# First two groups' maxima taken key part by key part; first keys and queries laid out ahead of the second keys

## What is computed

```python
q, k, v = (t.reshape(B, S, 16, 16) for t in (ln(x) @ Wq.T, ctx @ Wk.T, ctx @ Wv.T))   # 2048 queries, 1601 keys, 256 wide
scores = q k^T / 4, masked keys and future keys (key > query) at -inf
context = nan_to_num(softmax(scores)) @ v
x = x + (sigmoid(ln(x) @ Wg.T + bg) * context) @ Wo.T
x = x + sum over 8 experts of top-2 gated silu(xs @ w1) * (xs @ w3) @ w2,   xs = gate * ln(x)
```

## Time and profile before

| | |
|---|---|
| median of 3 runs | 688.75 us (688.59 to 693.32) |
| the profiled execution | 690.36 us, its span 688.6 us |
| mean granted PE clock of it | 0.963 |
| PE, DVE, ACT, POOL busy | 653.8, 469.9, 385.0, 242.9 us |

### The profile page before, as it was taken

The page is one execution under the profiler, slowest core; times in us unless marked ns, Lnnn a source line. Parts: engine busy times, 40 slices in busy tenths (PEclk is TensorE's granted clock), DMA queues, the critical chain, the costliest instruction groups (busy, mean ns, idle before and its releaser), DMA issues.

```text
span 688.6 us, 13557 instructions
## 1 busy us (share of the span) xinstructions
PE 653.8 (95%) x5320; PEld 377.0 (55%) x5320; DVE 469.9 (68%) x969; ACT 385.0 (56%) x778; POOL 242.9 (35%) x293
## 2 busy tenths in 40 slices
PE   7897999999989999999999999999999996899996
PEld 3354455455545445444554445545456675688884
DVE  5684778999866999989987975454423354645452
ACT  2212676766634777777566877677875640232331
POOL 5004123422140305020211614527164535566563
PEclk9898999999996999999999999999999998899997
DMA  6984766010700000000770101003010011012000
GB/s 169 242 118 84 130 129 79 2 21 33 114 11 1 3 3 2 2 33 32 96 181 1 35 1 31 2 3 108 2 44 21 16 33 62 31 62 90 34 31 30
DMA packets 29305, 36.58 MB, mean 53 GB/s; under 512 B 5833, under 2 KB 16457, under 8 KB 29242
## 3 DMA queue, kind: packets, MB, share of 16 engines
q1 hardware_dynamic: 26248, 34.53, 23.7%
q10 hardware_dynamic: 946, 0.92, 0.4%
q0 software_dynamic: 2048, 0.27, 0.3%
HBM read 25.58 MB, written 8.06 MB: 49 GB/s over the span
## 4 chain that ended last, share of the span: by engine, by line
PE 74%; POOL 9%; DVE 7%; issue 6%; ACT 4%; POOLq 0%; ACTq 0%; DVEq 0%
PE bank L1566 18%; PE bank L1544 14%; PE bank L1511 11%; PE bank L1395 11%; PE bank L1630 3%; POOL h_lo L1022 3%; POOL v_sb L1018 3%; PE bank L1632 2%; PE bank L1631 2%; DVE pmax L1284 2%; POOL xn_sb L994 2%; ACT probs L1150 2%; PE bank L1515 2%; DVE v_sb L1374 2%; PE bank L1470 2%
## 5 line engine op out<-in xcount | busy, mean ns | idle before, releaser
L1284 DVE TENSOR_REDUCE pmax<-bank 128x1 f32<-128x512 f32 (+6 forms) x640 | 327.5, 578 | 69.3 <-PE bank L1515 46.8
L1150 ACT ACTIVATE probs<-bank 128x512 f32<-128x512 f32 (+4 forms) x592 | 287.4, 545 | 138.0 <-PE bank L1544 86.8
L1566 PE MATMUL bank<-probs,vaug 128*32 128x256 f32 (+4 forms) x2048 | 156.1, 396 | 0.5 <-ACT probs L1150 0.5
L1544 PE MATMUL bank<-qaug,kaug 64*128 64x512 f32 (+4 forms) x592 | 149.0, 452 | 7.0 <-DVE pmax L1284 3.2
L1511 PE MATMUL bank<-kaug,qaug 62*128 62x512 f32 (+6 forms) x640 | 139.6, 414 | 3.1 <-DVE pmax L1284 1.6
L1544 PEld LDWEIGHTS bank<-qaug,kaug 64*128 64x128 f32 (+1 forms) x592 | 64.4, 185 | 82.3 <-ACT probs L1150 29.8
L1511 PEld LDWEIGHTS bank<-kaug,qaug 62*128 62x128 f32 x640 | 70.7, 189 | 56.5 <-DVE pmax L1284 21.3
L1032 POOL TENSOR_SCALAR nmax<-rmax 128x16 f32<-128x16 f32 x16 | 5.2, 323 | 235.3 <-DVE rmax L1292 235.3
L1566 PEld LDWEIGHTS bank<-probs,vaug 128*32 128x32 f32 (+1 forms) x2048 | 46.5, 109 | 52.1 <-issue 31.1
L1202 ACT ACTIVATE h_hi<-v_sb 128x512 fp32r<-128x512 f32 x32 | 20.2, 632 | 80.5 <-DVE v_sb L1374 79.4
L1022 POOL TENSOR_TENSOR h_lo<-v_sb,h_hi 128x512 fp32r<-128x512 f32 x32 | 41.2, 1288 | 61.3 <-ACT h_hi L1202 61.3
(11 more groups left out here) (137 smaller groups left out, 790.2 us busy)
## 6 DMA issues: line engine op xcount, KB each, us to landing
qaug<-s_dram SPq DMA_DIRECT2D x32, 256.0 KB, 3.3
qaug<-q_parts SPq DMA_DIRECT2D x18, 256.0 KB, 9.2
q_parts<-stage SPq DMA_DIRECT2D x7, 512.0 KB, 2.9
k_parts<-stage SPq DMA_DIRECT2D x4, 512.0 KB, 5.3
w_sb<-in_w SPq DMA_DIRECT2D x4, 512.0 KB, 11.0
out<-x_sb SPq DMA_DIRECT2D x8, 256.0 KB, 2.2
ctx_sb<-in_ctx_t SPq DMA_DIRECT2D x3, 512.0 KB, 5.7
x_sb<-in_x SPq DMA_DIRECT2D x3, 512.0 KB, 6.9
```

Of the source, the lines that this page charges most:

```text
L1150: act.activation(probs[0:rows, u % NSLOT, h, off:CH], bank_of(e)[0:rows, off:CH], ACT.Exp, scale=DK ** -0.5).then_inc(act_read, 1)
L1284: dve.tensor_reduce(pmax[:, n % 2, qt, h, slot:slot + 1], bank[:, 0:w], AX_X, ALU.max).then_inc(dve_read, 1)
L1544: last.append(pe.matmul(pair[side][0][0:r, off:CH], keys_at(b, ROWS, hp, P * j, r), qaug[b:b + ROWS, p % 2, hp, off:CH], start=True, stop= ...
L1566: last = pe.matmul(psum[O_BANK][32 * h:32 * h + 32, q0:q1], vaug[0:r, col:col + 32], probs[0:r, u % NSLOT, h, q0:q1], start=(j == 0), stop ...
```

## The change

Three edits. `max_pieces` sorts the pieces of groups 0 and 1 by slot: 16 pieces of keys 0 to 511, then 16 of the later keys. `projections(0)` has another order: query half 0 directly after the transposes, the `sel` of key chunk 0 and of the queries, and only then `kq k01` and its `sel`. And the pieces of slot 0 no longer need, nor wait for, `sel` of key chunk 1; on PE the first piece waits for the `sel` of key chunk 0 and of the queries, and the first slot-1 piece for that of key chunk 1.

```diff
 def max_pieces(n):
...
-    return out
+
+    return sorted(out, key=lambda piece: piece[5]) if n < 2 else out
...
-        return [*norm, ("kq", "k", 0, 0), *turn, ("kq", "k", 0, 1), *select["k", 0], ("kq", "q", 0, c), *select["k", 1],
-                *select["q", c], ("kq", "k", 1, 0), ("kq", "k", 1, 1), ("kload", p), ("kq", "q", 1, c), ("qload", p), *values, *gate]
+        return [*norm, ("kq", "k", 0, 0), *turn, ("kq", "q", 0, c), *select["k", 0], *select["q", c], ("kq", "k", 0, 1),
+                *select["k", 1], ("kq", "k", 1, 0), ("kq", "k", 1, 1), ("kload", p), ("kq", "q", 1, c), ("qload", p), *values, *gate]
...
             if p == 0 and g < 2:
-                return [("sel", w, c, pair) for w, c in (("k", 0), ("k", 1), ("q", ORDER[0])) for pair in range(4)] + old
+                keys = ((0,), (0, 1))[max_pieces(e[1])[e[2]][5]]
+                return [("sel", w, c, pair) for w, c in (*(("k", k) for k in keys), ("q", ORDER[0])) for pair in range(4)] + old
...
                             for engine in ("act", "dve"):
-                                pe.wait_ge(*taken(sel_of[engine]))
+                                pe.wait_ge(*taken(sel_of["k", 0, engine]))
+                                pe.wait_ge(*taken(sel_of["q", ORDER[0], engine]))
...
+                    if e == second_keys:
+                        for engine in ("act", "dve"):
+                            pe.wait_ge(*taken(sel_of["k", 1, engine]))
```

More of the change, by code:

```diff
@@ L594, in build @@
     early_of = {engine: [e for e in early if consumer(e) == engine][-1] for engine in ("act", "dve")}
-    sel_of = {engine: [e for e in plan if e[0] == "sel" and consumer(e) == engine][-1] for engine in ("act", "dve")}
+    sel_of = {(*of, engine): [e for e in plan if e[:3] == ("sel", *of) and consumer(e) == engine][-1]
+              for of in (("k", 0), ("k", 1), ("q", ORDER[0])) for engine in ("act", "dve")}
+    second_keys = next(e for e in plan if e[0] == "mx" and max_pieces(e[1])[e[2]][5])
     feed_at = {e[1:]: i for i, e in enumerate([e for e in plan if e[0] == "y"])}
```

## The result

The changed kernel takes 708.14 us (707.47 to 708.96), the kernel before, run beside it, 691.04 (688.59 to 694.45); the ratio is 1.024, interval 1.020 to 1.029. That is 17 us slower, where 1.4 us less was forecast. Run again with the last experiments, the ratio was 1.025 (1.019 to 1.030). The profiled execution of the changed kernel has a span of 707.2 us.

What follows compares the result with a forecast made beforehand. PE was taken as the limit from some 70 us on. Terms 0.8 + 0 + 1.1 + 1.2 - 0.4 - 0.7 - 2.0 - 1.4 gave -1.4 us, 687.3 on the median of 688.75; range 682 to 693, chance 0.85.

Steps and rivals of the forecast that it cites:

- What bounds the kernel: Whole kernel: PE is the limit from some 70 us on; a maximum ready sooner is worth nothing by itself.
- What the planner does: After `kq k01`: 4 pieces before `sel k1`, PE idling +1.1 us; then `kq k10`, `kq k11`, 10 pieces, +1.2 us.
- The clock of the new order: Early projections and selections: durations carried over from the old order; `kq k10` and `kq k11` take 4.9 us, to 31.3.
- Theory D: Set up for the experiments: the low clock lies beside other waits and costs nothing; filling is within 1.5 us of the changed kernel.
- The first `st`: First scores, near 59 to 61 us: stall from 3.16 to about 1.2, -2.0 us; half the low clock saved, -1.4 us.
- Moved transfers: Stores of `k10` and `k11` issued some 2.5 us later, `kload` slips 0 to 2.5 us: costs nothing at group 2.
- The sum: All terms together: -1.4 us; +6.0 with every bound at its worst, -7.2 at its best.
- the two gains of 0.4 and 0.7: Around the second query projection: 14 pieces done instead of 12, -0.4 us; PE's idle behind that projection goes, -0.7 us.
- the slower one named: Second query projection: DVE blocked while ACT waits for the store of `k10`; +3.3 us, 692; chance 0.20.
- The head start passes through: Up to the first turn of the maxima DVE is the limit; first piece 6.3 us earlier, gain 5 to 7 us, 682.5; chance 0.15.

Runs made afterwards that it cites:

- both cures: The changed kernel with the second-chunk key transfer held back until group 1's maxima rows landed, and idle products in PE's early waits and before the first `st`: ratio 0.996.
- the order alone: The changed kernel with the pieces unsorted again, so only the new order of projections and selections differs from the kernel before: ratio 1.001 (0.998 to 1.005).

## Why the prediction was wrong, point by point

*What bounds the kernel*: right. PE is the limit behind the start, and what was lost before stays: 17.9 us at group 6, 17.7 at group 15. A maximum that is ready sooner was worth nothing by itself: with both cures group 1 closed at 78.41 instead of 82.69, and the kernel was no faster than the old one with its waits filled (0.996 and 0.995).

*What the planner does*: right to the step. 4 pieces ahead of `sel k1`, then `kq k10`, `kq k11`, 10 pieces, `kload`. The wait ahead of the query projection was 0.78 us (+0.8 forecast), that ahead of `sel k1` 1.50 (+1.1). The order was right; the durations in it were not.

*The clock of the new order*: the first step that failed. I carried the durations of the old order over, "at a clock like the old one". The clock fell behind the idle stretch from 9 to 11 us in both kernels. In the old one it came back by the selections; in the new one, which has one more wait at 12.4 and another of 0.80 between the selections, it did not before 23.6. That these two waits hold it down is not shown singly, since they were filled together with the others. Nor is the clock of this stretch (12.2 to 23.5) the same in each execution: 0.81, 0.81, 0.89 and 1.00 in four profiles with the old order and unfilled waits, 0.50, 0.50, 0.50 and 0.70 in four with the new. `kq k10` and `k11` ended near 37.0 and not at 31.3, and the second query projection stood at 40.96 and not at 35. Group 0 closed 6.0 us late. Filled with idle products the same order gave back 12 us. But the kernel before gained 3.6 us from fills too, so of the 17 us between the two kernels an estimated 6 to 8 are the clock: 12 - 3.6 = 8.4, or 9.3 (from 1.0095 to 0.996) - 3.6 = 5.7 with the transfer held back. The transfer is 10, and 1 to 3 are left for the order itself: with the transfer held back and waits filled it stays 0.9 us behind the old kernel with two waits filled, and 3 behind it with five. That is about the 17. Theory D is out for this kernel. For the order alone, on the other hand, it is nearly right: the same low clock cost about 1 us there. What a low clock costs depended on what else was late.

The page "TensorE: Matmul & The Clock Gate" of the Trainium skill, section "HAM oscillation — how this bites in real kernels", tells of idle stretches of the matrix engine that make what follows start cold. The runs agree: with products in the waits the clock of 12.20 to 23.50 went from 0.50 to 1.00.

*The first `st`*: half right. The turn of group 0 fell behind `v` 5, and PE's wait was 2.02 us, between the 3.16 of before and the 1.2 forecast: 1.1 us gained of the 2.0. The 1.4 us for the clock did not come, it was 0.67 from 70 to 80. And this `st` ran at 68.70, not at 59 to 61, since all ahead of it was late.

*Moved transfers*: the second and larger failure, a term put at nothing. I priced a moved transfer by who waits for it, and wrote of group 2 "this costs nothing there". That was true, and not the question. `kload(1)` slid by 14 us, from 76.03 to 90.11, by the plan's own dependence on the norm and the projections of the next chunk, and so came to lie just ahead of four small DMAs on another queue. The trace of before had shown what a full set of DMA engines does: the two stores of 28.26 took 7.6 us to land, the stores of queries over the whole run 2.9. I worked out the first `kload` and never the second. It cost 10 us in the changed kernel (taking it out) and 13.5 us in the old one (putting it in), 10.7 of them behind group 1 in the profile.

*The sum*: its worst case was +6.0 us, and that already left out the two gains of 0.4 and 0.7. The measured +17 lies beyond it because neither failure had a bound in it: no bound was worked out for the clock of the first 40 us, and none for the second `kload`.

*The rivals*: the slower one named was DVE blocked behind the second query projection. It didn't happen in the changed kernel: ACT took that projection at 42.96, at once when PE had it, since PE itself was late. It is real all the same, and stands in the timeline of the kernel before with its waits filled (DVE idle 4.04 us). The slower side came by another mechanism, and the chance of 0.07 for it was too small. "The head start passes through" was seen only in runs with the start filled, as far as group 1.

## What to carry to other kernels

When an order is changed, follow every transfer of the plan that moves, for two chunks ahead, and ask not only who waits for it but which small transfers it now lies in front of. Where small row transfers lie on a chain, as here, try to hold the large one back until they have landed, and look at which loads stand behind it in its queue. Don't carry over durations of matmuls to a new order without asking which clock they will find: put idle products into the waits of both kernels first, and compare the orders then. And before a group that closes earlier is called a head start, ask what work was put off behind it.

## What the runs showed of the hardware

Four DMAs of 4 KB, issued on POOL's queue 1.2 to 3.2 us behind six of 256 KB on SP's, took 11.0 to 12.3 us to land (medians) instead of 2.8, in three kernels (the changed one, filled or not, and the old one with the transfer moved). The changed kernel has a second such meeting: the rows of group 2, issued at 126.0 behind six query loads issued from 120.46, took 11.3 us instead of 1.9, and PE did not wait for them. The page "DMA: Bandwidth & Descriptors" of the Trainium skill, section "Issuing engines are not separate DMA queues", says that DMAs of all issuing engines run on the same 16 DMA engines and interleave. The runs agree that the two queues share them. But they interleave late in the changed kernel: the DMA share was full up to 102, the rows had no packet in the first 8 us after their issue, and three quarters of their packets ran after 102. Why they came so late stays open.

A wait of PE of 2.4 us was followed in one execution by 20 us at a mean clock of 0.67 and in another, with the same steps at the same place, by 10 us at 0.80 and 10 at 0.86. Over four profiles with the same steps and the same wait, the stretch from group 5 to group 6 took 43.07 to 48.82 us. So the same wait can cost up to some 6 us more in one execution than in another.
